# Strided convolution: TensorE works as four 64x64 tiles on ten of 16 rows, VectorE on six, and batch 0 is written straight into the clustering's array

## The reference, cut to what matters

```python
c2 = sx.shape[1] // 2
x = jax.lax.conv_general_dilated(sx, w_down, window_strides=(2, 2), padding=((1, 1), (1, 1)),
                                 feature_group_count=c2, dimension_numbers=('NCHW', 'OIHW', 'NCHW'))
xx = jax.lax.stop_gradient(x[0].reshape(c, h * w))
mn = xx.min(axis=1, keepdims=True)
mx = xx.max(axis=1, keepdims=True)
xs = (xx - mn) / jnp.maximum(mx - mn, 1e-12)
labels = _kmeans_labels(xs)                     # 10 iterations and a last assignment
...
v5 = jnp.einsum('bchw,ck->bkhw', x, soh / jnp.maximum(scnt, 1.0)[None, :])
mu, var = _gmm_fit(wa)                          # 10 EM iterations on v5
y = jax.nn.sigmoid(jnp.einsum('bkn,kn->bk', box, w_conv))
gate = y[:, slabel]
pre_up = gate[:, :, None, None] * x + x
up = jnp.repeat(pre_up, 2, axis=1) * w_up[None, :, None, None]
return _bilinear_up_x2(up) + sx                 # then layer 1: upfirdn, leaky ReLU, upfirdn
```

## Time and profile before

| | |
|---|---|
| median of 3 runs | 7448.8 us |
| the profiled execution's own time | 7447.51 us |
| its span | 7445.7 us |
| TensorE busy | 6961.8 us (94%) |
| VectorE busy | 5924.4 us (80%) |
| ScalarE busy | 4571.4 us (61%) |
| GpSimd busy | 2522.2 us (34%) |
| mean granted TensorE clock | 0.967 of 2.4 GHz |
| DMA, moved in all | 891.87 MB, 120 GB/s on average |

### The profile page before, as it was taken

One profiled execution on the slowest core, in us unless ns is written; L12 is line 12 of the kernel. 1 busy time (PEld: TensorE's weight loads), 2 busy tenths in 40 slices (PEclk: granted clock), 3 DMA queues, 4 the chain that ended last, 5 costly groups with the idle time before them and its releaser, 6 DMA issues.

```text
span 7445.7 us, 691936 instructions
## 1 busy us (share of the span) xinstructions
PE 6961.8 (94%) x302277; PEld 6350.0 (85%) x302277; DVE 5924.4 (80%) x11620; ACT 4571.4 (61%) x9038; POOL 2522.2 (34%) x3076
## 2 busy tenths in 40 slices
PE   6699994079999999999999999999999999999999
PEld 2444442069999999999999999999999999999998
DVE  7399998967777777777777777777777777777776
ACT  0100001347777777777777777777777777777776
POOL 0000000034444444444444444444444444444443
PEclk9699997589999999999999999999999999999999
DMA  6188883023333333333333333333333333333332
GB/s 262 47 320 321 320 319 134 0 69 96 99 96 98 96 98 97 98 96 98 97 97 97 97 97 97 97 97 98 97 98 96 98 96 98 96 99 96 99 96 82
DMA packets 1261249, 891.87 MB, mean 120 GB/s; under 512 B 184336, under 2 KB 1234960, under 8 KB 1244432
## 3 DMA queue, kind: packets, MB, share of 16 engines
q1 hardware_dynamic: 1249936, 856.58, 37.2%
q10 hardware_dynamic: 11264, 34.61, 1.7%
HBM read 587.94 MB, written 303.04 MB: 120 GB/s over the span
## 4 chain that ended last, share of the span: by engine, by line
PE 79%; issue 0%; DVE 0%; DMA 0%; POOL 0%; SPq 0%; ACT 0%; DVEq 0%; POOLq 0%
PE bank L1087 26%; PE bank L1082 25%; PE twin L1082 14%; PE twin L1087 13%; PE twin L1221 2%; DVE x_sum L1319 0%; DMA img<-in_x 0%; DVE leaky L1295 0%; DMA low<-conv_dram 0%; POOL img L1041 0%; DVE up L1304 0%; SPq L993 0%; ACT dn L1286 0%; SPq L994 0%; ACT res L1271 0%
## 5 line engine op out<-in xcount | busy, mean ns | idle before, releaser
L1295 DVE SCALAR_TENSOR_TENSOR leaky<-bank,slope_t 128x512 f32<-128x512 f32 x4096 | 2630.8, 683 | 909.8 <-ACT slope_t L1255 909.8
L1082 PE MATMUL bank<-up_t,up 64*64 64x133 f32 x65536 | 2757.6, 276 | 2.4 <-issue 1.5
L1087 PE MATMUL bank<-down_t,leaky 64*64 64x35 f32 (+1 forms) x131072 | 2295.9, 221 | 13.4 <-issue 11.4
L1087 PEld LDWEIGHTS bank<-down_t,leaky 64*64 64x64 f32 x131072 | 2260.6, 135 | 23.8 <-issue 15.0
L1255 ACT ACTIVATE slope_t<-bank 128x512 f32<-128x512 f32 x4096 | 2225.7, 599 | 1.9 <-PE bank L1082 1.9
L1082 PEld LDWEIGHTS bank<-up_t,up 64*64 64x64 f32 x65536 | 2026.9, 133 | 3.6 <-issue 3.5
L1050 POOL TENSOR_TENSOR low_d<-low_v 128x252 f32<-128x252 f32 x512 | 310.9, 607 | 4820.2 <-ACT low_v L1277 4820.2
L1319 DVE SCALAR_TENSOR_TENSOR x_sum<-lift,coef,img 128x128 f32<-128x128 f32 x4096 | 1439.7, 411 | 13.5 <-POOL img L1041 13.5
L1271 ACT ACTIVATE res<-twin 128x512 f32<-128x512 f32 x1024 | 612.0, 598 | 1326.8 <-PE twin L1087 1326.8
L1082 PE MATMUL twin<-up_t,x_sum 64*64 64x133 f32 x32768 | 1395.6, 281 | 7.2 <-DVE x_sum L1319 5.3
L1087 PE MATMUL twin<-down_t,dn 64*64 64x35 f32 (+1 forms) x65536 | 1364.0, 221 | 7.1 <-issue 6.8
(11 more groups left out here) (159 smaller groups left out, 1787.6 us busy)
## 6 DMA issues: line engine op xcount, KB each, us to landing
img<-in_x SPq DMA_DIRECT2D x1024, 256.0 KB, 2.9
out<-res SPq DMA_DIRECT2D x1024, 256.0 KB, 2.4
rows_next<-in_x SPq DMA_DIRECT2D x42, 4224.0 KB, 13.9
rows_next<-in_x SPq DMA_DIRECT2D x14, 4096.0 KB, 13.5
low<-conv_dram SPq DMA_DIRECT2D x1024, 32.0 KB, 2.2
conv_dram<-conv_next ACTq DMA_DIRECT2D x56, 512.0 KB, 4.1
rows_in<-in_x SPq DMA_DIRECT2D x6, 4224.0 KB, 14.0
rows_in<-in_x SPq DMA_DIRECT2D x2, 4096.0 KB, 29.7
```

The source lines that it names most:

```text
L1082: return pe.matmul(acc[cols(c), a:b], src[cols(rt), cols(c)], up_t[cols(rt), a:b], start=first, stop=False, skip_group_check=True)
L1087: return pe.matmul(acc[cols(c), a:b], src[cols(rt)], down_t[cols(rt), k, a:b], start=first, stop=False, skip_group_check=True)
L1295: v.scalar_tensor_tensor(out=leaky[1 - m % 2][:, e, i].rearrange("p k w -> p (k w)"), in0=u2_acc[e][i][:], scalar=GAIN, in1=slope_t[e][i][ ...
```

## The change

- `V_ROWS` goes from 9 to 6. VectorE does six rows of each unit, TensorE ten.
- TensorE does its ten rows as four tiles of 64x64 instead of one array of 128x128 (`conv_on_tiles`). Tile (r, c) takes the channels of half r (64 partitions in, 64 x 64 weights of the diagonal matrix) and five of the ten rows (c), and writes them to partitions of half c of bank `2 * (n % 2) + r`. Each tap is four matmuls of 320 columns instead of one of 448. A unit now takes two banks, so the averaging moves from banks 2 and 3 to banks 4 and 5.
- ScalarE copies four pieces of 64 partitions x 320 elements instead of one of 128 x 448 (`copy_from_tiles`).
- `xx` is allocated before `first_convolution`, whose output tiles are now slices of it. The two `conv` tiles and the waits for their stores go; the stores to `conv_dram` stay. `clusters` no longer loads `xx`.
- In `other_convolutions` TensorE's unit gets one more wait, for a semaphore that has long been set (`ready`), and computes its two register values ahead of its waits.

```diff
-V_ROWS = 9
+V_ROWS = 6
 T_ROWS = QR - V_ROWS
+C_ROWS = T_ROWS // 2
...
+        def half(i):
+            return slice(HALF * i, HALF * (i + 1))
+
+        def conv_on_tiles(pe, rows_in, cb, n):
+            for s, (i, kh, kw) in enumerate(order):
+                for c in range(2):
+                    for r in range(2):
+                        acc = bank[2 * (n % 2) + r][half(c), 0:C_ROWS * WO].rearrange("p (r w) -> p r w", r=C_ROWS)
+                        src = conv_in(rows_in, n, i, kh, kw, V_ROWS + C_ROWS * c, V_ROWS + C_ROWS * (c + 1))
+                        mm = pe.matmul(acc[:, :, (1 if kw == 0 else 0):],
+                                       diag[half(r), cb * TAPS + (i * 3 + kh) * 3 + kw, half(r)], src[half(r)],
+                                       start=(s == 0), stop=(s == TAPS - 1), skip_group_check=True)
+            return mm
+
+        def copy_from_tiles(tile, n):
+            for c in range(2):
+                for r in range(2):
+                    ins = nc.scalar.activation(tile[half(r), V_ROWS + C_ROWS * c:V_ROWS + C_ROWS * (c + 1), :].rearrange("p r w -> p (r w)"),
+                                               bank[2 * (n % 2) + r][half(c), 0:C_ROWS * WO], ACT.Copy)
+            return ins
...
-                conv = [sb(f"conv{i}", [P, QR, WO]) for i in range(2)]
+                tiles = [xx[:, n % CB, n // CB * QR * WO:(n // CB + 1) * QR * WO].rearrange("p (r w) -> p r w", r=QR) for n in range(UB)]
...
-                        acc = bank[n % 2][:, 0:T_ROWS * WO].rearrange("p (r w) -> p r w", r=T_ROWS)
-                        for s, (i, kh, kw) in enumerate(order):
-                            mm = pe.matmul(acc[:, :, (1 if kw == 0 else 0):],
-                                           diag[:, cb * TAPS + (i * 3 + kh) * 3 + kw, :],
-                                           conv_in(rows_in, n, i, kh, kw, V_ROWS, QR), start=(s == 0), stop=(s == TAPS - 1),
-                                           skip_group_check=True)
-                        mm.then_inc(t_done, 1)
+                        conv_on_tiles(pe, rows_in, cb, n).then_inc(t_done, 1)
...
-                        nc.scalar.activation(conv[n % 2][:, V_ROWS:, :].rearrange("p r w -> p (r w)"),
-                                             bank[n % 2][:, 0:T_ROWS * WO], ACT.Copy).then_inc(t_copied, 1)
+                        copy_from_tiles(tiles[n], n).then_inc(t_copied, 1)
...
-                @block.sync
-                def _(sp):
-                    for cb in range(CB):
-                        sp.dma_start(xx[:, cb, :], conv_dram[cb * P:(cb + 1) * P]).then_inc(xx_loaded, 16)
...
-            first_convolution()
             xx = own.enter_context(nc.sbuf_tensor("xx", [P, CB, PX], F32))
+            first_convolution(xx)
```

42 lines of the change are left out of this document (16 added, 26 removed).

## The result

| | before | after |
|---|---|---|
| median | 7449.12 us (4 runs, 7448.55 to 7454.62) | 7370.47 us (4 runs, 7368.92 to 7372.22) |
| the profiled execution's span | 7445.7 us | 7370.3 us |

The ratio is 0.9893, 95% interval [0.9876, 0.991]: 79 us faster. The forecast was 7290 us with 7265 to 7345 around it, so 159 us faster. About half of that came, and the time lies outside the range. The computing operations have the durations that were forecast for them. What missed is how load and work fit together (loads are longer, and TensorE runs some us of every second unit at half clock), and one block that nobody touched.

A forecast was written before the change was run, and what follows sets the result against it. VectorE and TensorE were taken as both full, 15.17 us a convolution unit, the load next. First block 19 + reload 12.5 + other 56 units 128 - 0.6 = 159 us off 7447.5: 7290 us, range 7265 to 7345.

The forecast's parts named there:

- VectorE, TensorE, ScalarE: Convolution unit's work: VectorE 11.6 us, TensorE 10.1 us plus 0.57 us of averaging, ScalarE's four copies 1.75 us.
- The lower bound for a pass: TensorE's four-tile pass of 320 columns: 0.27 us if the tiles run side by side, from `resample`'s records.
- Rival C: Convolution on TensorE: column tiles share one input stream, a pass takes 0.54 us, 7742 us in all; chance 6%.
- The period: Convolution units: two buffer chains of load plus work in turn, (14.15 + 11.6)/2 = 12.9 us a unit.
- the other units: The 56 units of `other_convolutions`: last ends at 1074.8 us instead of 1202.7, 128 us less.
- I am wrong if: Signs in the convolution: passes 0.3 us or more apart, overlapping loads clearly over 14.2 us, or mid-block clock below 1.00.
- TensorE's clock: Convolution blocks: idle gaps of 1.6 and 2.8 us per pair of units; the sum counts no cold starts.
- Rival A: Convolution: clock falls in the gaps, work 12.2 us, period 13.2 us, 19 us more, 7309 us; chance 13%.
- First block: First convolution block: unit 7 ends at 139.5 us instead of 158.8, 19 us less.
- Reload: Between the convolution blocks: the two loads of `xx` and VectorE's wait ahead of the minimum go, 12.5 us less.
- `resample`: Resampling block, its code untouched; the forecast's sum has no term for it.
- DMA rate: Convolution loads: the skill's 358 GB/s would give 13.5 us a unit, about 7328 us; the trace's 391 and 434 GB/s disagree.

The follow-up runs named there:

- eight rows: Changed kernel with eight rows on VectorE and eight on TensorE instead of six and ten: 7415.92 us.
- 14 taps: Kernel before, with only the first 14 of the 18 taps computed on both engines: 7355.35 us.
- half the load: Changed kernel, loading only the first of two input channels from the fifth unit of each block on: 7239.95 us.
- the fillers' run: Changed kernel with four unused matmuls of 512 columns on TensorE behind every unit of `other_convolutions`: 7444.82 us.
- The filler matmuls: Changed kernel with three unused matmuls of 512 columns on TensorE behind odd units only: 7371.29 us.
- the pad of 67 instructions: Kernel before with 134 waits on a long-set semaphore (67 instructions) ahead of the mixture's work on TensorE: 7477.37 us.
- the pad of 32: Changed kernel with 64 waits on a long-set semaphore (32 instructions) ahead of the mixture's work on TensorE: 7355.62 us.
- the load split: Changed kernel with each load split by channel, each half started once both engines are through with that channel's taps: 7255.1 us.
- 36 instructions on ScalarE: Kernel before with 72 waits on a long-set semaphore (36 instructions) on ScalarE in the other convolutions' block: 7450.12 us.

## Why the prediction was wrong, by its own steps

- **VectorE, TensorE, ScalarE.** Right: 619 ns for 618, a warm unit of 10.42 us for 10.1, copies of 432 ns for 438. The lower bound for a pass (0.27 us, from `resample`) was the nearer one. Rival C, shared column streams, didn't happen.
- **The period, the step that failed.** The formula held: two chains in turn, each a load and a unit's work. With the means of the even units (those behind the long wait), 15.4 us from issue to VectorE's start and 12.5 us of work, it gives (15.4 + 12.5)/2 = 13.95, and 13.89 was measured; the odd units come to the same with 16.3 and 11.6. With eight rows it gives 14.55 for a measured 14.51, and for the even stretch with 14 taps (14.2 + 12.0)/2 = 13.1. With half the load, (9.5 + 11.5)/2 is below the work, and the work, 11.6, is the period. What was wrong are its two terms. The load chain went in with 14.15 us, read in a kernel in which next to nothing depended on it, and was 15.4; work went in with 11.6 and was 12.5, the cold start being counted at nothing. Both together are 1.0 us a unit, and 54 units of that are the 54 us by which the other units fell short (74 instead of 128).
- **Why the load was longer.** Two of the three signs under "I am wrong if" came true, a load clearly over 14.2 us once it overlaps with others and a clock below 1.00 in the middle of the block. Overlapping is the smaller part of the load's growth, 0.2 us (15.2 in the fillers' run, at nearly the period of before, to 15.4) to 0.4 (13.9 to 14.3 with 14 taps). The rest, 1.1 us or more, was not thought of at all. That the change multiplies TensorE's matmuls stood in the order of before and after, and the packets of code move on the same DMA engines that carry the load: with a packet among its data a load took 15.2 to 15.3 us, with the packet behind it 13.9 to 14.1.
- **TensorE's clock.** Rival A for every second unit, the case for which the text had half of 19 us. The gap was argued away with "the longer work shortens the gap that caused it". It doesn't. The text split TensorE's idle time into 1.6 and 2.8 us; in the trace nearly all of it lies in one gap, 4.0 us (median) ahead of the even units, and the odd units follow at once behind the late, cold ones. VectorE's wait ahead of even units was 3.4 us (median). A cold unit costs 1.6 us of TensorE, 12.02 - 10.42, and 0.5 (median) to 0.9 us (mean) of the pair's work, since VectorE's unit would have ended at 11.6. The filler matmuls got 0.26 us a unit back, 11.6 us by the start of `resample`. The Trainium skill, TensorE: Matmul & The Clock Gate, "HAM oscillation — how this bites in real kernels", describes waits for DMA after which each burst of matmuls begins cold. For every second unit the trace agrees: clock 0.50 at 632 to 634 us, 12.02 us for a unit instead of 10.42.
- **First block.** 15.3 us instead of 19: the same load of 15.4 us and three cold starts, in a block of eight.
- **Reload.** 12.5 us as forecast.
- **`resample`.** 26.5 us, a third of what was missing. It was counted at nothing because its code doesn't change. Its code doesn't; its place does. That a shift alone can cost this much is shown by the pad of 67 instructions in the kernel before, 7477.37 - 7450.61 = 27 us; in the changed kernel the pad of 32 takes 15 of the 26.5 us away again. No pad tried there gave back all 26.5.
- **DMA rate.** Rightly not taken for a ceiling. The Trainium skill's 358 GB/s (DMA: Bandwidth & Descriptors, "Specifications") gives an estimate of 13.5 us a unit, which is near the 13.89 that came, by coincidence: with the load split the same bytes come every 11.8 us, 415 GB/s over 600 us, so the measurement decides against it. The Trainium skill, DMA: Bandwidth & Descriptors, "Measured (HBM→SBUF, 128 partitions, SWDGE, issued from GpSimd)", has 425 GB/s for a core whose neighbour is idle, and the 415 GB/s of this run are near that.

The sum: 3.7 + 54 + 26.5 = 84 us, and 159 - 75.4 = 83.6 is what was missing. The mechanism of the period was right; two of its terms, the load chain and the work, were too small, and the block behind the convolution was taken as fixed.

## What to carry to other kernels

When a change takes a kernel from bound by work to bound by a two-buffer load, the period is half of load plus work, and both terms have to be taken as they will be in the new state: the latency read where next to nothing waited for it was 1.2 us too short here. The way out is not faster work but an earlier start: freeing half a buffer at half of the unit turned 79 us of gain into 194. And four times the instructions cost twice here: their packets delayed the loads, and they moved the loop behind them. A difference of some tenths of a per cent in an untouched loop should be tried with a pad before it is explained.

## What the runs showed of the hardware that I had not expected

- The time of an unchanged loop of TensorE depends on where it lies in TensorE's code: pairs of 11.460, 11.483, 11.513, 11.531 and 11.549 us for the same instructions, up to 45 us of 7450. Which property of the place counts is open. 36 instructions on ScalarE change nothing.
- Four 64x64 tiles take 0.29 us for a pass of 320 strided columns in float32, with two different input streams over the same partitions (10.42 us for 36 passes). The two streams don't take turns: for that the prediction's estimate was 0.54 us a pass.
- Packets of code share the DMA engines with data: 16 KB, 0.95 us each, 57 instead of 6 in 600 us. A load of 4224 KB with one among its data took 15.2 to 15.3 us, with one behind its data 13.9 to 14.1 (eleven loads of one run).
- One core moved 415 GB/s for 600 us while its engines computed.
